# The context's value projections as three fp32r products of high and low parts

## The reference, cut to what matters

```python
x = x + tanh(g_xattn[0]) * L0_xattn(layernorm(x), ctx)
x = x + tanh(g_ffn[0])   * L0_ffn(layernorm(x), w0)
x = x + tanh(g_xattn[1]) * L1_xattn(layernorm(x), ctx, mask)
x = x + tanh(g_ffn[1])   * L1_ffn(layernorm(x), ...)          # router, 32 experts
x = x + tanh(g_xattn[2]) * L2_xattn(layernorm(x), ctx, ...)   # k = ctx @ Wk, v = ctx @ Wv (256 x 512)
x = x + tanh(g_ffn[2])   * L2_ffn(layernorm(x), ...)
x = x + tanh(g_xattn[3]) * L3_xattn(layernorm(x), ctx, ...)   # cross part: k, v of the context (256 x 1024)
x = x + tanh(g_ffn[3])   * L3_ffn(layernorm(x), ...)
```

## Time and profile before

| | |
|---|---|
| runs, us | 1424.66, 1426.15, 1432.83 (median 1426.15) |
| span of the profiled execution, us | 1419.7 (its own time is not given apart from the runs) |
| busy, share of the span | PE 92%, DVE 72%, ACT 57%, POOL 48% |
| chain that ended last, by engine | PE 64%, DVE 15%, issue 7%, ACT 7%, POOL 5%, DMA 3% |
| mean granted clock of TensorE | 0.980 |

### The profile page before, as it was taken

One profiled execution on the slowest core, in us unless ns is written; L12 is line 12 of the kernel. 1 busy time (PEld: TensorE's weight loads), 2 busy tenths in 40 slices (PEclk: granted clock), 3 DMA queues, 4 the chain that ended last, 5 costly groups with the idle time before them and its releaser, 6 DMA issues.

```text
span 1419.7 us, 23324 instructions
## 1 busy us (share of the span) xinstructions
PE 1310.6 (92%) x7218; PEld 1092.3 (77%) x7218; DVE 1020.8 (72%) x2214; ACT 814.6 (57%) x2024; POOL 676.4 (48%) x701
## 2 busy tenths in 40 slices
PE   5988999998799999989999799999988999999994
PEld 3546888886588888878888478888867788888884
DVE  7787656666787878756556577878888787877754
ACT  6754222233566666674222567776777778776353
POOL 1010455553344444416651245666567867665444
PEclk9997999999999999999999999999999999999898
DMA  6221555563200000011110395001120001114283
GB/s 226 89 97 46 170 168 179 178 173 105 74 9 23 8 16 1 1 37 46 45 44 9 116 335 172 1 1 31 31 82 31 31 31 60 31 42 175 77 292 125
DMA packets 68499, 121.00 MB, mean 85 GB/s; under 512 B 6901, under 2 KB 36233, under 8 KB 67884
## 3 DMA queue, kind: packets, MB, share of 16 engines
q1 hardware_dynamic: 65563, 114.46, 25.0%
q0 software_dynamic: 2256, 4.24, 0.8%
q10 hardware_dynamic: 576, 1.05, 0.2%
HBM read 82.56 MB, written 39.12 MB: 86 GB/s over the span
## 4 chain that ended last, share of the span: by engine, by line
PE 64%; DVE 15%; issue 7%; ACT 7%; POOL 5%; DMA 3%; POOLq 0%; ACTq 0%; SPq 0%; DVEq 0%
PE ps L1381 9%; PE ps L1515 7%; PE ps L1488 7%; PE ps L1325 6%; PE ps L1533 6%; PE ps L1466 5%; PE ps L1395 5%; PE ps L1498 4%; PE ps L1186 3%; PE ps L1341 3%; POOL urs L937 3%; PE ps L1477 3%; DVE usum L2925 2%; ACT probs L2121 1%; DMA rows_out<-tile_y,tile_to 1%
## 5 line engine op out<-in xcount | busy, mean ns | idle before, releaser
L944 POOL TENSOR_TENSOR probs<-probs,prec 128x512 f32<-128x512 f32 x192 | 202.4, 1054 | 305.2 <-DVE prec L2957 305.2
L2121 ACT ACTIVATE probs<-ps,nmax 128x256 f32<-128x256 f32 x384 | 178.8, 472 | 201.0 <-DVE nmax L2950 201.0
L1488 PE MATMUL ps<-k_feat,q_feat 128*128 128x256 f32 x768 | 198.4, 381 | 2.7 <-ACT q_feat L2112 1.9
L1515 PE MATMUL ps<-probs_t,v_tok 128*128 128x256 f32 x768 | 197.7, 380 | 0.2 <-ACT ob L2140 0.2
L937 POOL TENSOR_TENSOR urs<-uve,neg_half 128x4 f32<-128x4 f32 x136 | 136.9, 1007 | 54.0 <-DVE uve L2926 43.1
L1488 PEld LDWEIGHTS ps<-k_feat,q_feat 128*128 128x128 f32 x768 | 136.8, 190 | 16.8 <-issue 3.5
L2950 DVE TENSOR_REDUCE nmax<-ps 128x2 f32<-128x512 f32 x192 | 131.3, 684 | 24.2 <-PE ps L1488 21.7
L1498 PE MATMUL ps<-ident,probs 128*128 128x128 f32 x768 | 116.5, 274 | 26.2 <-ACT probs_t L2130 24.8
L1515 PEld LDWEIGHTS ps<-probs_t,v_tok 128*128 128x128 f32 x768 | 130.9, 190 | 10.6 <-ACT probs_t L2130 0.4
L1498 PEld LDWEIGHTS ps<-ident,probs 128*128 128x128 f32 x768 | 91.3, 140 | 61.6 <-issue 33.2
L2130 ACT ACTIVATE probs_t<-ps 128x512 f32<-128x512 f32 x192 | 115.4, 601 | 0.9 <-PE ps L1498 0.9
(11 more groups left out here) (421 smaller groups left out, 3667.8 us busy)
## 6 DMA issues: line engine op xcount, KB each, us to landing
rows_in<-zero_rows SPq DMA_DIRECT2D x3, 5200.0 KB, 35.5
tile_w<-in_l3f_w SPq DMA_DIRECT2D x21, 385.5 KB, 6.8
w<-in_l1f_w SPq DMA_DIRECT2D x24, 256.0 KB, 5.1
spread_w<-we_dram SPq DMA_DIRECT2D x16, 384.0 KB, 3.7
kv_cross<-kv_out SPq DMA_DIRECT2D x20, 256.0 KB, 2.0
kv_first<-kv_out SPq DMA_DIRECT2D x16, 256.0 KB, 2.0
spread_w<-we_dram SPq DMA_DIRECT2D x16, 256.0 KB, 4.2
w<-in_l2f_w SPq DMA_DIRECT2D x8, 512.0 KB, 3.5
```

The source lines that it names most:

```text
L944: pool.tensor_tensor(p3, p3, spread(prec[g % 3][:, :], [P, TB, S]), ALU.mult)\
L1488: mm = pe.matmul(ps[g % 2][:, j * S:(j + 1) * S], q_feat[:, h, j * P:(j + 1) * P], k_feat[:, kv, :], start=True, stop=True)
L1515: mm = pe.matmul(ps[6][:, 0:S], v_tok[:, tb, kv * P:(kv + 1) * P], probs_t[g % 2][:, tb, :], start=tb == 0, stop=tb == TB - 1)
L2121: ins = act_e.activation(probs[g % 4][:, j, :], ps[g % 2][:, j * S:(j + 1) * S], ACT.Exp, bias=nmax[g % 3][:, j:j + 1], accum_out=psums[g ...
```

## The change

GpSimd splits the context and the value weights between the first norm's four calls of line 917 and the second's. `context_split(b)` waits for `c_out` and writes `c_high` (fp32r) in two products with `ones_col`, 128x256 each, and `c_low` in one difference, 128x512. `values_weights(i)` waits for `kv_w_in` (32 for the third layer, 64 for the fourth) and makes, per 128x512 piece, one product and one difference: 2 pieces for i = 0, 4 for i = 1. A value unit on TensorE waits for `c_split` and `values_split` and makes six fp32r products in place of two fp32 ones. Key units stay as they were.

New tiles take room that the later weights of the first attention layers use after the prologue. Some semaphores are merged: `cq_turned` into `c_turned`, `cq_out` into `c_out`, `c_whole` into `c_rounded`, `whole_rounded` into `rounded`, with their counts raised; ScalarE's unused step counter goes.

```diff
+            c_high = sb("c_high", [P, KB, NTOK], F32R, where=a)
+            c_low = sb("c_low", [P, KB, NTOK], F32R, where=a)
+            values_high = [sb(f"values_high{i}", [P, KB, (i + 1) * HALF], F32R, where=a) for i in range(2)]
...
-            part_scales(4 * B)
+            def context_split(b):
+
+                pool.wait_ge(c_out, b + 1)
+                for kb in range(KB):
+                    here = (slice(None), kb, slice(b * S, (b + 1) * S))
+                    st.mark(pool.tensor_tensor(c_high[here], c_feat[here], ones_col[:, :].to_broadcast([P, S]),
+                                               ALU.mult))
+                st.wait()
+                here = (slice(None), slice(None), slice(b * S, (b + 1) * S))
+                pool.tensor_tensor(c_low[here], c_feat[here], c_high[here].bitcast(F32), ALU.subtract)\
+                    .then_inc(c_split, 1)
+
+            def values_weights(i):
+
+                pool.wait_ge(kv_w_in, 32 * (i + 1))
+                raw, low = wsets[i]["v"], (w_high, w_low)[i]["v"]
+                for kb in range(KB):
+                    for n in range(i + 1):
+                        here = (slice(None), kb, slice(n * HALF, (n + 1) * HALF))
+                        st.mark(pool.tensor_tensor(values_high[i][here], raw[here],
+                                                   ones_col[:, :].to_broadcast([P, HALF]), ALU.mult))
+                        st.wait()
+                        ins = pool.tensor_tensor(low[here], raw[here], values_high[i][here].bitcast(F32),
+                                                 ALU.subtract)
+                ins.then_inc(values_split, 1)
+
+            part_scales(B)
+            for b in range(B):
+                context_split(b)
+            for i in range(2):
+                values_weights(i)
+            part_scales(3 * B)
...
+                    terms = [(c_feat, w)]
+                    if what == "v":
+                        later = int(i >= len(KV_FIRST))
+                        pe.wait_ge(c_split, b + 1)
+                        pe.wait_ge(values_split, later + 1)
+                        high, low = values_high[later], (w_high, w_low)[later]["v"]
+                        terms = [(c_high, high), (c_high, low), (c_low, high)]
                     for kb in range(KB):
-                        mm = pe.matmul(banks[i % 2][:, :], c_feat[:, kb, b * S + j * P:b * S + (j + 1) * P],
-                                       w[:, kb, n * HALF:(n + 1) * HALF], start=kb == 0, stop=kb == KB - 1)
+                        for q, (c, w) in enumerate(terms):
+                            mm = pe.matmul(banks[i % 2][:, :], c[:, kb, b * S + j * P:b * S + (j + 1) * P],
+                                           w[:, kb, n * HALF:(n + 1) * HALF], start=kb == 0 and q == 0,
+                                           stop=kb == KB - 1 and q == len(terms) - 1)
                     mm.then_inc(kv_ready, 1)
...
-                pe.wait_ge(c_whole, b // 2 + 1)
+                pe.wait_ge(c_rounded, 2 + b // 2 + 1)
```

More of the change, by code:

```diff
@@ L274, in build @@
         with ExitStack() as a:
+            sb("c_split_hold", [P, 64 * 256], where=a)
+            c_high = sb("c_high", [P, KB, NTOK], F32R, where=a)
+            c_low = sb("c_low", [P, KB, NTOK], F32R, where=a)
+            values_high = [sb(f"values_high{i}", [P, KB, (i + 1) * HALF], F32R, where=a) for i in range(2)]
+        with ExitStack() as a:
             wo_raw = sb("wo_raw", [P, HEADS, D], where=a)
@@ L483, in build @@
         gate_ready = sem("gate_ready")
-        dve_step, pool_step, act_step = sem("dve_step"), sem("pool_step"), sem("act_step")
+        dve_step, pool_step = sem("dve_step"), sem("pool_step")
         source_step_done, round_step_done = sem("source_step_done"), sem("round_step_done")
@@ L490, in build @@
                                                        sem("scaled_in"))
-        rounded, quantised, whole_rounded = sem("rounded"), sem("quantised"), sem("whole_rounded")
+        rounded, quantised = sem("rounded"), sem("quantised")
         part_turned, part_out, prod_ready, x_added = (sem("part_turned"), sem("part_out"), sem("prod_ready"),
@@ L494, in build @@
         c_turned, c_out, c_scaled, cz_ready = sem("c_turned"), sem("c_out"), sem("c_scaled"), sem("cz_ready")
-        c_rounded, cq_turned, cq_out, c_whole = sem("c_rounded"), sem("cq_turned"), sem("cq_out"), sem("c_whole")
+        c_rounded = sem("c_rounded")
         w0_by_vector, w0_by_scalar, w0_turned = sem("w0_by_vector"), sem("w0_by_scalar"), sem("w0_turned")
         max_in, max_out = sem("max_in"), sem("max_out")
-        kv_w_in = sem("kv_w_in")
+        kv_w_in, c_split, values_split = sem("kv_w_in"), sem("c_split"), sem("values_split")
         kv_ready, kv_copied, stored = sem("kv_ready"), sem("kv_copied"), [sem(f"stored{i}") for i in range(4)]
@@ L516, in build @@
                            "gated_ready", "prod_done", "hi_ready", "act_ready",
-                           "y_ready", "y_added")}
+                           "y_ready", "y_added") if not (f is L1F and k == "y_added")}
         fs["l3f"] = {**fs["l2f"], "w13_hi": sem("l3f_w13_hi"), "w2_hi": sem("l3f_w2_hi")}
@@ L1206, in turn_context_blocks @@
                 if b >= 2:
-                    pe.wait_ge(cq_out, b - 1)
+                    pe.wait_ge(c_out, B + b - 1)
                 for kb in range(KB):
@@ L1212, in turn_context_blocks @@
                                           ident[:, :])
-                mm.then_inc(cq_turned, 1)
+                mm.then_inc(c_turned, 1)
             def turn_first(b):
@@ L1218, in product_first @@
             def product_first(b):
-                pe.wait_ge(cq_out, b + 1)
+                pe.wait_ge(c_out, B + b + 1)
                 product(0, b, h_feat, lambda kb: cq_feat[:, kb, b * S:(b + 1) * S])
@@ L1266, in _ @@
             pe.wait_ge(w0_by_scalar, 2)
-            pe.wait_ge(cq_out, B)
+            pe.wait_ge(c_out, 2 * B)
             for kb in range(KB):
@@ L1287, in _ @@
             for b in range(B):
-                turn_part(2, b, z[:, :].rearrange("p (t d) -> p t d", d=D), whole_rounded, b + 1)
+                turn_part(2, b, z[:, :].rearrange("p (t d) -> p t d", d=D), rounded, 2 * B + b + 1)
                 if b < 2:
                     early(1)
-                pe.wait_ge(c_whole, b // 2 + 1)
+                pe.wait_ge(c_rounded, 2 + b // 2 + 1)
                 product(2, b, q_whole, lambda kb: cq_whole[:, b * TB + kb, :])
@@ L1770, in _ @@
             act_e = sc_eng
-            st = Steps(act_e, act_step)
             def block(t2, g):
@@ L1861, in context_blocks_out @@
             def context_blocks_out(b):
-                act_e.wait_ge(cq_turned, b + 1)
+                act_e.wait_ge(c_turned, B + b + 1)
                 for i in range(TB):
@@ L1868, in context_blocks_out @@
                                                scale=csc[:, g:g + 1])
-                ins.then_inc(cq_out, 1)
+                ins.then_inc(c_out, 1)
             kv_done = [0]
@@ L2494, in context_whole @@
             def context_whole(half):
-                v.wait_ge(cq_turned, 2 * half + 2)
+                v.wait_ge(c_turned, B + 2 * half + 2)
                 here = slice(half * NT // 2 * D, (half + 1) * NT // 2 * D)
@@ L2499, in context_whole @@
                 link(v.tensor_scalar(cz[:, here], flat[0], crc[:, 16:17], FP8_MAX, ALU.mult, ALU.min))
-                whole_e4m3(cz[:, here], cm[:, here], flat[1]).then_inc(c_whole, 1)
+                whole_e4m3(cz[:, here], cm[:, here], flat[1]).then_inc(c_rounded, 1)
             def first_scales():
@@ L2529, in whole_round @@
                                      FP8_MAX, ALU.mult, ALU.min))
-                whole_e4m3(zz, quarter(m, b), zz).then_inc(whole_rounded, 1)
+                whole_e4m3(zz, quarter(m, b), zz).then_inc(rounded, 1)
             def first_low(c):
```

## The result

The changed kernel takes 1436.7 us (median of 6 runs, 1435.0 to 1438.2) where the kernel before takes 1426.04 beside it (1424.6 to 1432.8): a ratio of 1.0058, 95% interval 1.0042 to 1.0075. (Ratios in this text are estimated from the single runs of both kernels and are not the quotients of two medians; here that quotient is 1.0075.) It is slower, by 6.0 to 10.7 us. In a second series the same program gave 1429.62 against 1423.6, ratio 1.0039 (1.0025 to 1.0053). The forecast was 6.9 us.

What follows compares the result with a forecast made beforehand. TensorE was taken to bound 32.3 to 64.2 us, mostly VectorE from 66.9. Projections -3.1, TensorE's lateness +9.2 and clock +0.75 made +6.9 us on the median 1426.15: 1433.0 us, range 1424 to 1439.

Steps and rivals of the forecast that it cites:

- The hold on VectorE: First norm, 14.19 to 27.45 us: GpSimd's splits hold VectorE off, making it 13.0 us late with the rounded context.
- the rival by which they are not: First norm: VectorE's small instructions are not held, only wide ones wait; +2.5 us, 1428.7 us; chance 17%.
- the one without a hold on the path: First norm: VectorE loses under 3.8 us up to 27.45, leaving only the projections' gain; 1423.0 us; chance 13%.
- The picture of a strict alternation: First norm: VectorE and GpSimd take turns, all 27 VectorE instructions held, each of 20 GpSimd instructions holding VectorE once.
- The room of 3.8 us: TensorE turns the rounded context 3.8 us after VectorE has it, so 13.0 us of lateness becomes 9.2.
- The clock's +0.75 us: Around TensorE's context turn: a longer pause puts the whole key unit at the lower clock, 0.75 us more.
- The gain of 3.1 us: TensorE's projections, 40.45 to 62.50 us: nine value units on the chain each save 0.34 us.
- the rival with 17%: 67 to 85 us: shorter units leave TensorE gaps and the lower clock; +4.3 us more, 1437 us; chance 17%.
- one of my signs of being wrong: A granted TensorE clock at 0.5 between 50 and 107 us would show the forecast wrong.
- The sum: By the end of the norms: -3.1 + 9.2 + 0.75 = +6.9 us, carried over to the median.
- the forecast's case: Whole kernel: VectorE's hold outweighs the projections' gain; 1433.0 us, on its own 1429 to 1437; chance 53%.

Runs made afterwards that it cites:

- Experiment 1: Changed kernel with all GpSimd splits, but each value unit two fp32 products again: 1431.8 us, ratio 1.0058 to the kernel before.
- experiment 4: Changed kernel with fp32 value units and half the splits: context's only 1431.0 us, ratio 1.0018; value weights' only 1434.08 us, ratio 1.0042.
- the weights run: Changed kernel with only the value weights' 12 splits on GpSimd and fp32 value units: 1434.08 us, ratio 1.0042 to the kernel before.
- experiments 4, 5: The latter: changed kernel with only the context's splits, fp32 value units, ScalarE's first key unit copy moved ahead of the second z: 1428.96 us, ratio 1.0001.
- products-only run: Changed kernel without splits, value units of six fp32r products on constant tiles: 1419.58 us, ratio 0.9975 to the kernel before.

## Why the prediction was right

**The hold on VectorE** was the deciding term: 20 GpSimd instructions, each costing its length less 0.30, make c_rounded 13.0 us late. It came at 40.81, 13.4 late. Small instructions are held too, as the rows above show, so the rival by which they are not is out; so is the one without a hold on the path. The picture of a strict alternation, in which each of VectorE's instructions is held, is too simple: 8 of the 27 keep their length. But GpSimd's 20 instructions cost what the count says, since the 19 held ones lose 13.0 us. Experiment 1 shows that the splits make the loss without the new products, and experiment 4 that the count works for half of the work too, short by 0.5 to 1.1 us. Why a GpSimd instruction gives back 0.30 us was not tested apart.

**The room of 3.8 us** was right for the sum and wrong as a picture. TensorE was 9.6 us late (forecast 9.2) because VectorE's path is the longer one at 13 us of lateness, and so it is at 9.6 (the weights run). I took TensorE's arrival at 31.25 for fixed, and it is not: the same hold moves it, through into, ScalarE's queue and the bank of the third key unit. With a third of the hold, 4.1 us, VectorE's own path would cost 0.3 us, and this other one costs 2.7 (experiments 4, 5). I had followed VectorE's late results to TensorE alone, and not to ScalarE, whose queue holds copies behind a wait for VectorE.

**The clock's +0.75 us** in the prologue: the key unit behind the turn took 3.18 us for 2.69, and the turn 1.12 for 0.85, together 0.76. That the sum fits is luck in part: I had given all of it to the key unit, which ran only partly at the lower level, and nothing to the turn.

**The gain of 3.1 us** is the term that was mis-sized. I counted nine value units on the chain. With shorter units six are left on it, both in the changed kernel and in the products-only run: behind the fifth, ScalarE becomes the chain, where TensorE was before, so that shorter units there give nothing. Six times 0.34 is 2.0, and on top of the splits 1.9 are measured by 74.6 us. That the products alone reached 3.1 by the first expert product was luck: 2.4 by cz, and 0.7 behind it, from units that I had put at nothing. The sum by then is +7.7 for the 6.9: the splits alone have cz 9.6 late, and 1.9 go off.

**The clock's second fall** is the rival with 17%, and it came in part, in both profiles of the changed kernel: one value unit on the chain behind a pause, at 2.56 instead of 1.38. It was one of my signs of being wrong, a granted clock at 0.5 at about that place (I had said between 50 and 107 us, it came in 104 to 108). The price was 1.2 us and not 4.3, since the turn-and-product pairs between 75 and 93 us, which I had priced, kept their clock (the chain of waits has the product there at 1.97 us before and after).

**The sum**: 6.9 forecast; 8.2 at the first expert product in the first pair of profiles and 7.0 in the second; 6.0 to 10.7 from the first series' times, 3.6 to 7.5 from the second's. The median of the first, 1436.7, is nearer to the rival's 1437 than to 1433.0; by mechanism it is the forecast's case and a quarter of the rival (1.2 of its 4.3 us). Two errors partly hid behind each other in the total: a gain 1.2 us too large by the norms' end against 0.8 us of TensorE's lateness that was taken up before cz (9.6 and 0.76 late at the turn and the key unit, 9.6 at cz).

## What to carry to other kernels

An engine that stands idle is free only if its work shares nothing with the bottleneck. Before moving work to GpSimd, count the VectorE instructions beside it that read two SBUF operands or are tensor_scalars, small ones included, and charge each GpSimd instruction nearly in full. Follow a late result to every engine that waits for it and to what stands behind the wait in that engine's queue, since slack measured at one consumer is not slack when the same delay reaches it by a second way. A TensorE clock regained in one stretch need not show in the time: here it fell again behind the next pause. And count the units on the chain again after making them shorter, since another engine may take the chain over.

## What the hardware showed that I had not expected

- A memset holds a 128x4 tensor_scalar for its whole length (1.31 us for 0.17), and one tensor_scalar waited for two memsets in a row, 2.43 us.
- A value unit in fp32r is 1.38 us at the upper clock and 2.46 to 2.56 where the granted clock had fallen.
- Between the norms' end and 108 us the granted clock fell once in each of the six profiles with fp32r value units, at the one place or some 30 us later, and in neither profile of the kernel before. Single profiles differ by 0.5 to 1.2 us through this.
- TensorE's first products after its first pause can run at half speed (a step of 0.85 instead of 0.43 us, three to five times) with the granted clock at 1.00 in those windows. This is not the half pace behind the later pause of experiment 4, which has a granted clock of 0.50. It differs between executions of one kernel and moves the first norm by up to 2 us, so single profiles can't be compared there to better than that.
